# Counting the first pair of tiles inside the message loop, and row statistics ahead of the one-hot steps, in a graph-network plus expert-router kernel

## What is computed

```python
loop = jnp.arange(N); src = concat([src, loop]); dst = concat([dst, loop])
dis = rsqrt(degree(dst))
norm = dis[src] * dis[dst]
for l in range(2):
    x_res = x
    h = x @ W[l]
    agg = segment_sum(norm[:, None] * h[src], dst) + b[l]
    x = relu(agg + x_res @ resW + resb)
```

## Time and profile before

| what | value |
|---|---|
| median of three runs | 1909.43 us |
| the profiled execution | 1904.65 us, of it a span of 1902.9 us from the first to the last instruction |
| TensorE busy | 1817.4 us, 96% of the span |
| VectorE busy | 1124.6 us, 59% |
| ScalarE busy | 853.9 us, 45% |
| mean granted TensorE clock | 0.984 of 2.4 GHz |
| first block, to ScalarE's last instruction | 0 to 171.85 us |
| pair 0 counted by itself | 175.11 to 194.30 us |

### The profile page before, as it was taken

The page is one execution under the profiler, slowest core; times in us unless marked ns, Lnnn a source line. Parts: engine busy times, 40 slices in busy tenths (PEclk is TensorE's granted clock), DMA queues, the critical chain, the costliest instruction groups (busy, mean ns, idle before and its releaser), DMA issues. The chain is left out here.

```text
span 1902.9 us, 35412 instructions
## 1 busy us (share of the span) xinstructions
PE 1817.4 (96%) x11170; PEld 1119.2 (59%) x11170; DVE 1124.6 (59%) x2789; ACT 853.9 (45%) x1822; POOL 341.2 (18%) x347
## 2 busy tenths in 40 slices
PE   4787999999999999999999999999999999999996
PEld 3576555555555555555544444444444478888885
DVE  7787666766666666666514444444444567555553
ACT  2366565656555565655512222222222232556562
POOL 1582000000000000000001111111111124333332
PEclk9898999999999999999999999999999999999998
DMA  7257999898999999985285544444445479324441
GB/s 235 76 118 151 327 299 333 294 293 267 319 259 309 276 364 320 363 311 198 104 341 183 188 183 179 179 179 179 179 180 185 177 236 331 112 76 122 140 139 52
DMA packets 135978, 416.70 MB, mean 219 GB/s; under 512 B 13685, under 2 KB 81611, under 8 KB 129640
## 3 DMA queue, kind: packets, MB, share of 16 engines
q1 hardware_dynamic: 90376, 255.13, 38.2%
q0 software_dynamic: 45392, 160.65, 27.9%
q10 hardware_dynamic: 144, 0.13, 0.0%
HBM read 162.27 MB, written 262.07 MB: 223 GB/s over the span
## 5 line engine op out<-in xcount | busy, mean ns | idle before, releaser
L1404 PE MATMUL bank<-parts,counts 128*128 128x512 f16 x4704 | 1157.8, 379 | 0.9 <-DVE sums L1425 0.9
L1404 PEld LDWEIGHTS bank<-parts,counts 128*128 128x128 f16 x4704 | 415.9, 97 | 357.9 <-issue 2.5
L1559 ACT ACTIVATE counts<-bank 128x392 f16<-128x392 f32 x800 | 394.8, 497 | 314.8 <-PE bank L1479 308.0
L623 DVE TENSOR_TENSOR rows<-rows,iota_lo 128x2048 bf16<-128x2048 bf16 x200 | 245.0, 1225 | 236.0 <-PE bank L1479 235.5
L1479 PEld LDWEIGHTS bank<-rows 128*128 128x128 bf16 x3200 | 229.6, 99 | 204.5 <-issue 27.4
L1479 PE MATMUL bank<-rows 128*128 128x98 bf16 x3200 | 280.5, 212 | 11.7 <-DVE rows L623 10.9
L623 DVE TENSOR_TENSOR rows<-rows,iota_hi 128x1568 bf16<-128x1568 bf16 x200 | 193.7, 968 | 0.0
L467 POOL DMA_INDIRECT first_rows<-route_rows,route_spot_i x49 | 47.8, 976 | 604.5 <-DVE tokens L458 405.0
L1419 ACT ACTIVATE middle<-bank 128x256 f32<-128x256 f32 x98 | 37.1, 380 | 186.8 <-PE bank L1404 172.1
L2187 PE MATMUL bank<-y_t,counts 128*128 128x256 f32 x480 | 115.3, 384 | 3.3 <-ACT y_t L2259 3.3
L2187 PE MATMUL bank<-h_t,counts 128*128 128x256 f32 x480 | 113.7, 380 | 0.0
(11 more groups left out here) (268 smaller groups left out, 1764.0 us busy)
## 6 DMA issues: line engine op xcount, KB each, us to landing
counts_table<-counts SPq DMA_DIRECT2D x25, 3136.0 KB, 15.1
counts<-counts_table SPq DMA_DIRECT2D x24, 3136.0 KB, 11.6
first_rows<-zero_rows POOLq DMA_DIRECT2D x3, 10530.0 KB, 57.6
second_rows<-zero_rows POOLq DMA_DIRECT2D x3, 10449.0 KB, 66.4
first_out<-zero_rows POOLq DMA_DIRECT2D x3, 10368.0 KB, 49.1
res_tile<-res_table SPq DMA_DIRECT2D x98, 128.0 KB, 7.1
first_rows<-zero_rows POOLq DMA_DIRECT2D x1, 10270.0 KB, 58.0
second_rows<-zero_rows POOLq DMA_DIRECT2D x1, 10191.0 KB, 63.2
```

Source lines behind the costliest of these rows:

```text
L623: return nc.vector.tensor_tensor(rows, k, v, ALU.is_equal)
L1404: mm = nc.tensor.matmul(acc[:, 0:2 * dim], lhs, rhs, start=s == 0, stop=s == tiles)
L1559: nc.scalar.activation(counts[:, b, :, :].rearrange("p s (o n) -> p o s n", o=2)[:, :, :, q * QUAD:(q + 1) * QUAD], bank[4 + q % 4][:, 0:Q ...
```

## The change

The change does two things. In the order rows of the changed kernel below, the line numbers are its own.

**Pair 0.** Its one-hot rows, quads and copies move from the main block into the message loop of the first block. TensorE's `count_quad` follows the messages of tiles 25 to 46, one or two quads behind each (`quads_after`), in two PSUM banks (6 and 7). ScalarE's `quad_copy` stands behind high(t) and middle(t-1) and takes the quads that followed message t-1. VectorE's eight one-hot steps (`pair_heads`, `pair_tiles`) stand behind the remainders of tiles 15 to 18 and 28 to 43. In the main block the sums of pair 0 come first, with 12 products ahead of the first quad of pair 1. The flag's product moves to bank 5.

**Statistics.** `stats(3)` moves in front of `head_onehots(3)`, `stats(4)` in front of `head_onehots(6)`, and `stats(5)` to `stats(8)` to behind the residuals of tiles 16, 20, 26 and 32, where they stood behind 19, 24, 30 and 36.

```diff
+        STATS_AFTER = (16, 20, 26, 32)
+        FREE_AFTER = -(-tiles // 2)
+        COUNT_FOR = tiles - FREE_AFTER - 2
+        def quads_after(t):
+            return range(*(min(max(n, 0), COUNT_FOR) * quads // COUNT_FOR for n in (t - FREE_AFTER, t + 1 - FREE_AFTER)))
+        def quad_bank(q):
+            return bank[6 + q % 2]
+        ONEHOTS_AFTER_H = (15, 17) + tuple(FREE_AFTER + -(-(r - 1) * per_step * COUNT_FOR // quads) for r in range(2, steps))
 # ScalarE
+                def quad_copy(q):
+                    act.wait_ge(quad_ready, q + 1)
+                    nc.scalar.activation(
+                        counts[:, 0, :, :].rearrange("p s (o n) -> p o s n", o=2)[:, :, :, q * QUAD:(q + 1) * QUAD],
+                        quad_bank(q)[:, 0:QUAD * width].rearrange("p (n o s) -> p o s n", o=2, s=tiles), ACT.Copy).then_inc(quad_out, 1)
...
                         roots(2 + (9, 17, 27).index(t))
+                    for q in quads_after(t - 1):
+                        quad_copy(q)
 # TensorE
+                def count_quad(q):
+                    r, u0 = divmod(q * QUAD, STEP)
+                    if u0 == 0:
+                        pe.wait_ge(onehots_made, r + 1)
+                    if q >= 2:
+                        pe.wait_ge(quad_out, q - 1)
+                    for u in range(QUAD):
+                        at = (u0 + u) // 2
+                        mm = nc.tensor.matmul(quad_bank(q)[:, u * width:(u + 1) * width], pair_lo[:, r % 2, at, :, u % 2],
+                                              pair_hi[:, r % 2, at, :, u % 2], start=True, stop=True)
+                    mm.then_inc(quad_ready, 1)
...
+                        pe.wait_ge(keys_out, pairs - 1)
+                    for q in quads_after(t):
+                        count_quad(q)
 # VectorE
+                def pair_heads(r):
+                    if r >= 2:
+                        dve.wait_ge(quad_ready, (r - 1) * per_step)
+                    onehot_rows(pair_lo[:, r % 2, :, :, :], keys_t[:, 0, 1, r * STEP:(r + 1) * STEP], iota_lo, STEP, P)
+                def pair_tiles(r):
+                    onehot_rows(pair_hi[:, r % 2, :, :, :], keys_t[:, 0, 0, r * STEP:(r + 1) * STEP], iota_hi, STEP, width).then_inc(onehots_made, 1)
...
+                    if t in ONEHOTS_AFTER_H:
+                        pair_heads(ONEHOTS_AFTER_H.index(t))
+                    if t - 1 in ONEHOTS_AFTER_H:
+                        pair_tiles(ONEHOTS_AFTER_H.index(t - 1))
 # main block, TensorE
+        SUMS_AHEAD = 12
+                    ahead = SUMS_AHEAD if first else 0
+                    if first:
+                        sum_units(pe, b, i, i, 0, ahead, update.sums_out, update.sums_ready, first)
...
-                for q in range(quads):
-                    build(q, 0, True)
                 sum_pair(0, 0, True)
```

More of the change, by code:

```diff
@@ L608, in rows_of @@
             return table.rearrange("(t p) d -> p t d", p=P)
+        QUAD = 4
+        quads = P // QUAD
+        STEP = 16
+        steps = P // STEP
+        per_step = STEP // QUAD
         open_scope()
@@ L727, in gnn_moe_kernel @@
         middle_ready = sem("middle_ready")
+        onehots_made = sem("onehots_made")
+        quad_ready = sem("quad_ready")
+        quad_out = sem("quad_out")
         HEAD_STEPS = head_cols // HIST
@@ L994, in _ @@
                         pe.wait_ge(disorder_ready, 1)
-                        nc.tensor.matmul(bank[6][:, 0:3], ones[:, :], disorder[:, :], start=True, stop=True).then_inc(ones_summed, 1)
+                        pe.wait_ge(keys_out, pairs - 1)
+                        nc.tensor.matmul(bank[5][:, 2 * P:2 * P + 3], ones[:, :], disorder[:, :], start=True, stop=True).then_inc(ones_summed, 1)
+                    for q in quads_after(t):
+                        count_quad(q)
             @block.vector
@@ L1135, in flag_and_bounds @@
                     dve.wait_ge(ones_summed, 5)
-                    link(nc.vector.tensor_reduce(over[:, 0:1], bank[6][:, 0:3], AX, ALU.add))
+                    link(nc.vector.tensor_reduce(over[:, 0:1], bank[5][:, 2 * P:2 * P + 3], AX, ALU.add))
                     link(nc.vector.tensor_scalar(over[:, 0:1], over[:, 0:1], 1.0, None, ALU.min))
@@ L1166, in _ @@
                 stats(2)
+                stats(3)
                 head_onehots(3)
@@ L1183, in _ @@
                 starts()
[L1184 removed]
                 for t in range(16, tiles):
                     residual(t)
[L1187 to L1188 removed]
+                    if t in STATS_AFTER:
+                        stats(5 + STATS_AFTER.index(t))
                     if t == 22:
@@ L1469, in tensor, with build @@
             def tensor(pe):
-                def build(q, i, first):
+                def build(q, i):
                     r, u0 = divmod(q * QUAD, STEP)
@@ L1474, in build @@
                         pe.wait_ge(onehots_made, i * steps + (r + 1))
-                    if not (first and q < 4):
-                        pe.wait_ge(quad_out, i * quads + (q - 3))
+                    pe.wait_ge(quad_out, i * quads + (q - 3))
                     for u in range(QUAD):
@@ L1485, in sum_pair @@
                     units = LAST_UNITS if last else UNITS
+                    ahead = SUMS_AHEAD if first else 0
+                    if first:
+                        sum_units(pe, b, i, i, 0, ahead, update.sums_out, update.sums_ready, first)
                     for q in range(quads):
                         if not last:
-                            build(q, i + 1, False)
-                        sum_units(pe, b, i, i, q * units // quads, (q + 1) * units // quads, update.sums_out, update.sums_ready, first,
+                            build(q, i + 1)
+                        sum_units(pe, b, i, i, ahead + q * (units - ahead) // quads, ahead + (q + 1) * (units - ahead) // quads, update.sums_out, update.sums_ready, first,
                                   chunk_free=chunk_free if last else None)
@@ L1509, in vector, with rows_of_step @@
             def vector(dve):
-                def rows_of_step(r, i, b, first):
-                    if not (first and r < 2):
-                        dve.wait_ge(quad_ready, i * quads + (r - 1) * per_step)
+                def rows_of_step(r, i, b):
+                    dve.wait_ge(quad_ready, i * quads + (r - 1) * per_step)
                     nodes_of = slice(r * STEP, (r + 1) * STEP)
@@ L1524, in pair @@
                                           keys_t[:, bass.ds(i, 1), :, :].rearrange("p a k n -> p (a k n)")).then_inc(keys_copied, 1)
-                    dve.wait_ge(keys_copied, i + 1)
+                    dve.wait_ge(keys_copied, i)
                     for r in range(steps):
-                        rows_of_step(r, i, b, isinstance(i, int) and i == 0)
+                        rows_of_step(r, i, b)
                         if there(i * 2 - 4):
@@ L1542, in pair @@
                                 update.res_and_message(dve, i * 2 - 2, 0, i - 1)
-                for i in range(4):
+                for i in range(1, 4):
                     pair(i, i % 2)
```

17 lines of the change are left out of this document (7 added, 10 removed).

## The result

The changed kernel takes 1927.45 us (median of four runs, 1926.51 to 1932.36) against 1908.46 (1906.18 to 1910.65): a ratio of 1.0106, with a 95% interval of 1.0092 to 1.0119. It is slower by 19 us, where +9.6 was forecast. The direction and the kind of loss are as predicted; the size is twice as large, and 1927.45 lies at the very end of the range. The profiled execution took 1926.51 us.

What follows compares the result with a forecast made beforehand. TensorE, gapless from the main block on, makes the first sum's time decisive; ahead of it VectorE and TensorE wait in turn, then TensorE, then VectorE's one-hot rows set the pace. -19.0 - 8.8 + 2.4 + 35.0 = +9.6: 1919.0 us, range 1907 to 1928.

Steps and rivals of the forecast that it cites:

- part 1: Main block's start: the first sum needs nothing of the main block once pair 0 leaves it, -19.0 us.
- part 2: Residual loop: statistics first removes most of VectorE's 14.3 us of waiting, so message 0 comes earlier, -8.8 us.
- part 3: Messages 15 to 18: two one-hot steps on VectorE, 4.0 us less waits there, delay it by +2.4 us.
- the way in: Up to message 28: TensorE's lead is lost, so that message starts at 150.81 in place of 148.30, +2.5 us.
- exchanges: Messages 28 to 47: TensorE and ScalarE wait for each other around quad copies; 52.1 us in place of 20.1, +32.0.
- way out: Behind message 47: two quad copies stand behind high(47) on ScalarE, +0.5 us.
- the price of the exchange: Messages 28 to 46: one round of message, high, middle, quad copy and quad takes 2.65 us, against 1.06 a message.
- the second rival: Exchanges: TensorE's clock falls, each takes 1.05 us more, 18.9 in all; +28.5, 1938 us; 7 in 100.
- the third rival: First loop: statistics first gains nothing because VectorE meets another late producer; +18.4, 1928 us; 7 in 100.
- The first rival: Messages 28 to 47: copies get ahead of high(t), ScalarE's work sets the pace, 28.2 us; 1892 us, 8 in 100.

Runs made afterwards that it cites:

- run 3: Changed kernel with 16 unread matmuls on TensorE ahead of the first quad behind each message from tile 25 on: 1915.67 us, ratio 1.0050 to the kernel before.
- run 5: Kernel before with only the row statistics in the order of the change: 1906.58 us, ratio 1.0005.
- run 6: Kernel before with the statistics in the change's order and GpSimd's weight loads moved behind the main block's zero stores: 1900.97 us, ratio 0.9976.
- run 7: Kernel before with only GpSimd's weight loads moved behind the main block's zero stores: 1911.35 us, ratio 1.0028.
- run 9: Changed kernel with quad copies in front of high on ScalarE and VectorE's flag chain in four pieces: 1889.39 us, ratio 0.9914 to the kernel before.
- run 1: Changed kernel with ScalarE's quad copies in front of high(t) instead of behind middle(t-1): 1891.18 us, ratio 0.9922 to the kernel before.

## Why the prediction was wrong in size

The terms, each measured to the first sum on the two profiles:

| term | forecast | measured | how |
|---|---|---|---|
| part 1, pair 0 out of the main block | -19.0 | -21.4 | block's end to first sum, 22.45 to 1.04 |
| part 2, statistics | -8.8 | -9.65 | message 0, 118.81 to 109.16 |
| part 3 and the way in | +4.9 | +5.16 | message 0 to 28, 29.49 to 34.65 |
| exchanges | +32.0 | +44.57 | message 28 to 47, 20.10 to 64.67 |
| way out | +0.5 | +1.77 | message 47 to the block's end, 3.45 to 5.22 |
| sum | +9.6 | +20.44 | first sum, 194.30 to 214.74 |

Message 0 stands in the timeline of the kernel before:

```profile
118.81 8.81 PE L952 MATMUL bank<-both_w,counts 128*128 128x256 f32 x40
```

**The step that failed is the price of the exchange**, 2.65 us, which took the upper clock for granted: the second rival, the clock, was given only 7 in 100. The runs showed a mean clock of 0.59 in the exchanges, steps of 3.60 to 3.68 us once it had fallen, and +44.57 us in place of +32.0. The walk through the exchange was right: TensorE waits for a copy 19 times between message 28 and message 47, and at the upper clock the stretch costs 51.72 us (run 3) for 52.1. But the price took every matmul of the message from rows at the upper level. The rival was refused on one stretch of 2 us, where TensorE was busy 1.16 of 2.00 us at a clock of 1.00. The same view of the changed kernel:

```profile
150.00:152.00 2.00, 0.84 (x5) 0.47 (x3) 0.58 (x2) 1.34 (x5) 1.53 (x3) 1.00 1.02 95
152.00:154.00 2.00, 1.85 (x8) 1.59 (x9) 0.00 (x0) 0.48 (x2) 0.00 (x0) 0.50 1.06 125
...
156.00:158.00 2.00, 1.29 (x8) 0.84 (x8) 0.79 (x2) 0.64 (x2) 0.00 (x0) 1.00 0.82 146
...
160.00:162.00 2.00, 1.76 (x9) 1.28 (x8) 0.26 (x1) 0.77 (x3) 0.00 (x0) 0.50 1.09 154
```

A stretch like that of the earlier trace rows does stand at 1.00 here as well (150 to 152, 0.84 us busy). One window showed that the clock can stay up for a while under such a load, not that it stays up through nineteen such exchanges. The clock held for three, fell, came back once and stayed down from 160 to the first sums. The rival's 1.05 us for one exchange were right (tile 36: 3.68 us, and 2.62 in run 3). Its total of 18.9 was too high, and run 3 gives 12.95: the exchanges of tiles 28, 29, 30 and 32 ran at the upper level but for tenths of a microsecond, and those of tiles 35 and 39 took about as long in run 3 (3.68 and 3.56 us) as at the lower level. The way out belongs to the same cause: its last two messages took 3.74 us. In run 3 it took 4.01 us, from 201.13 to the end of the last middle at 205.14, near the 3.45 + 0.5 of the forecast.

The rule cited with that rival, from the Trainium skill, page "TensorE: Matmul & The Clock Gate", section "A second HAM failure mode: psum-queue depth-cycling", has the clock swing where groups cycle through PSUM banks with short idles; the trace agrees, with waits of at most 1.5 us and a mean clock of 0.59, though here the clock came back once only. The time lies between the prediction's sum and this rival's.

**Part 1 was short by 2.4 us, and part 2 right for a reason that was not in it.** The prediction says that GpSimd's fetches "stay off the path", and it has no term for the loads that follow them. In the kernel before those loads are on it: the block ends twice, once with the last middle and once, 2.3 us later, with GpSimd's queue (runs 5 to 7). So part 1 gained 2.3 us that the stretch behind the barrier does not show. Moving the message loop's end forward by 8 us gains nothing there (run 5). In the change the 9.65 us count only because the exchanges put the loop's end far behind GpSimd's. The sum of parts that were priced one by one came out near for these two, but the parts do not add in general: part 2 is worth 0 in the kernel before, about 10 behind the quads. So the third rival, that statistics first gain nothing, is true of the edit alone and false of the change, by a mechanism that it did not name. One reading in part 2, and in the description of the residual loop, is off by one: line 939 makes the product of tile t wait for the result of tile t-4, so it is product 37 that waits for residual 33. No term of the sum hangs on it.

GpSimd's rows in the trace of before end at 151.78, 20 us ahead of the last middle, so that it looks done in good time. The Trainium skill, page "Perfetto Trace Analysis", section "DMA Instruction — SWDGE (GPSIMD)", says that such a row ends when the descriptors are written, not when the data have moved; the trace agrees, with 20.3 us from issue to landing in run 5.

**The first rival** was rightly refused for the order as written: the circle is closed. Its 28.2 us and 1892 us are near what the kernel does once the order is turned round (27.98 in run 9; 1891.18 and 1889.39 us).

Of what the prediction said would show it, message 0, the waits at each step and the first sum next to VectorE's first instruction (0.06 us) came as told. The clock, the step of 2.65 us, and with them the block's end near 200 (213.70) and the first sum near 204 (214.74), did not.

## What to carry to other kernels

When a queue has few buffers, look at what stands in front of the copy that frees one: if it needs work that the waiting engine has yet to issue, the lead is lost at once, and putting the copy first (or the producer one step later) gives it back without a buffer. Price a chain of short waits on TensorE at both clock levels, and don't refuse the lower one on a single stretch that stayed up. Ahead of a barrier, list when each engine and each DMA queue ends; a gain is worth no more than the distance to the next one, and GpSimd's own loads held it here until they had landed and some 4 us more, long after its rows had ended.

## What the hardware showed that was not expected

- TensorE's granted clock fell to its lower level (0.50) in a chain of waits of 0.8 to 1.5 us, after three exchanges at 1.00, with TensorE busy 44.33 of 64.67 us. Sixteen matmuls of 128 columns in each wait kept it at 1.00 for 51.72 us.
- The barrier at the first block's end opened 0.98 us behind the last middle when GpSimd's queue was done (runs 1, 6, 7 and the changed kernel), and at 175.11, 175.81 and 177.35 us when the message loop ended first (the kernel before, runs 5 and 9; last loads issued by 151.78, 151.78 and 151.46). In the first two that is some 4 us more than the 20 us to landing; what fills these 4 us is not shown.
- Message 0 came between 109.07 and 113.68 us in eight profiles with the statistics first, and between 118.81 and 123.01 in three without: means of 111.4 and 121.6. Two profiles alone tell such a term to about 4 us.
